# Storing the last tile of a per-sequence low-rank update in two transfers: 108 rows and 20 rows for 128

## The reference

```
B_sel = B[adapter_ids]
A_sel = A[adapter_ids]
Bx = jnp.einsum('bni,bri->bnr', x, B_sel)
out = jnp.einsum('bnr,bor->bno', Bx, A_sel)
return out * SCALING        # SCALING = 16.0 / 16
x = x + _L0_cond_ref(x, A, B, itok_B_3_7)
```

## Time and profile before

| | |
|---|---|
| median of three runs | 91.9 us (91.75 to 92.27) |
| the profiled execution, its own time | 92.17 us |
| its span, first to last instruction | 90.4 us |
| busy share of the span | TensorE 90%, GpSimd 70%, VectorE 66%, ACT 66% |
| DMA | 34.82 MB in 9297 packets, mean 385 GB/s |
| granted TensorE clock, mean | 0.973 |

### The profile page before, as it was taken

The page is one execution under the profiler, slowest core; times in us unless marked ns, Lnnn a source line. Parts: engine busy times, 40 slices in busy tenths (PEclk is TensorE's granted clock), DMA queues, the critical chain, the costliest instruction groups (busy, mean ns, idle before and its releaser), DMA issues.

```text
span 90.4 us, 3583 instructions
## 1 busy us (share of the span) xinstructions
PE 81.4 (90%) x1451; PEld 61.7 (68%) x1451; DVE 59.7 (66%) x111; ACT 59.5 (66%) x154; POOL 62.9 (70%) x141
## 2 busy tenths in 40 slices
PE   3998999989999999999999999999999999989200
PEld 3997778748786878787878787786868687443000
DVE  0309968276595868777686959595959595999000
ACT  1339869939696969696969695968687776542200
POOL 6103992999999998979696979797969792800000
PEclk9999999999999999999999999999999999999955
DMA  1999999999999999999999999999999999997980
GB/s 27 315 401 419 415 406 415 401 413 406 406 410 410 402 424 413 406 419 417 413 421 413 422 413 410 415 422 406 421 417 413 421 410 397 406 383 314 408 335 24
DMA packets 9297, 34.82 MB, mean 385 GB/s; under 512 B 450, under 2 KB 962, under 8 KB 9282
## 3 DMA queue, kind: packets, MB, share of 16 engines
q1 hardware_dynamic: 7552, 27.79, 76.8%
q10 hardware_dynamic: 1730, 6.82, 18.6%
HBM read 17.83 MB, written 16.78 MB: 383 GB/s over the span
## 4 chain that ended last, share of the span: by engine, by line
PE 82%; DMA 6%; ACT 4%; issue 1%
PE t_bank L255 35%; PE bx_bank L268 21%; PE y_banks L288 18%; DMA x_all<-in_A 6%; PE y_banks L315 2%; PE t_bank L319 2%; ACT x_all L365 1%; PE bx_bank L319 1%; ACT b_table L369 1%; PE y_banks L242 1%; PE bx_bank L315 1%; ACT x_all L424 1%; ACT x_t L377 1%; PE t_bank L315 1%; PE bx_bank L242 0%
## 5 line engine op out<-in xcount | busy, mean ns | idle before, releaser
L465 DVE TENSOR_TENSOR x_all<-y_banks,x_all 128x1024 f32<-128x1024 f32 x29 | 35.5, 1225 | 15.4 <-PE y_banks L288 15.0
L377 ACT COPY x_t<-t_bank 128x512 f32<-128x512 f32 x64 | 34.4, 591 | 13.6 <-PE t_bank L255 12.8
L198 POOL CAST a_duo<-a_table 128x512 fp32r x64 | 36.6, 613 | 3.5 <-PE y_banks L288 1.8
L255 PE MATMUL t_bank<-ident,x_all 128*128 128x128 f32 x256 | 35.0, 280 | 0.4 <-ACT x_t L377 0.4
L255 PEld LDWEIGHTS t_bank<-ident,x_all 128*128 128x128 f32 x256 | 27.4, 141 | 7.4 <-issue 5.2
L188 POOL COPY b_duo<-b_table 128x256 f32 x64 | 22.8, 399 | 6.0 <-PE bx_bank L268 6.0
L268 PE MATMUL bx_bank<-x_t,b_duo 128*32 128x64 f32 x1024 | 20.8, 222 | 0.0
L268 PEld LDWEIGHTS bx_bank<-x_t,b_duo 128*32 128x32 f32 x1024 | 15.8, 109 | 5.4 <-issue 5.4
L288 PE MATMUL y_banks<-a_duo,bx_parts 64*128 64x512 f32 x112 | 17.3, 420 | 0.3 <-issue 0.3
L456 DVE TENSOR_TENSOR bx_parts<-bx_bank,bx_parts 32x64 fp32r<-32x64 f32 x64 | 14.1, 220 | 1.4 <-ACT bx_parts L392 0.3
L392 ACT CAST bx_parts<-bx_bank 32x64 fp32r<-32x64 f32 x64 | 13.0, 204 | 1.9 <-PE bx_bank L268 1.3
(11 more groups left out here) (31 smaller groups left out, 22.2 us busy)
## 6 DMA issues: line engine op xcount, KB each, us to landing
x_all<-in_x SPq DMA_DIRECT2D x5, 2048.0 KB, 28.6
out_y<-x_all ACTq DMA_DIRECT2D x3, 2048.0 KB, 15.4
x_all<-in_x SPq DMA_DIRECT2D x4, 1024.0 KB, 14.0
out_y<-x_all SPq DMA_DIRECT2D x1, 3072.0 KB, 14.0
out_y<-x_all SPq DMA_DIRECT2D x6, 512.0 KB, 4.7
x_all<-in_x SPq DMA_DIRECT2D x4, 512.0 KB, 7.2
out_y<-x_all SPq DMA_DIRECT2D x1, 2048.0 KB, 9.7
out_y<-x_all SPq DMA_DIRECT2D x2, 1024.0 KB, 6.7
```

What stands on the lines that cost most here:

```text
L198: last = nc.gpsimd.tensor_copy(a_duo[duo % 2][:, k, :], a_table[:, bass.ds(adapters[k] * BANK, BANK)])
L255: last = nc.tensor.transpose(t_bank[unit % 2][:, c * P:(c + 1) * P], x_all[:, 2 * duo + tile, at:at + P], ident[:, :])
L377: nc.scalar.copy(x_t[duo % 2][:, half * HALF:(half + 1) * HALF, tile, :], t_bank[unit % 2][:, :].rearrange("p (c n) -> p c n", c=HALF)).th ...
L465: nc.vector.tensor_tensor(here, product, here, ALU.add).then_inc(y_drained, 1)
```

## The change

The store of tile 31 is issued as two transfers, rows 0 to 107 and rows 108 to 127, one right after the other on SP's queue; all other stores stay as they are. The last wait counts one transfer more.

```
--- before.py
+++ after.py
@@ -46,6 +46,7 @@
     LOADS += [(t, t + 4) for t in range(10, 30, 4)] + [(30, TILES)]
     STORES_BY_ACT = {4: (0, 4), 7: (4, 8), 10: (8, 12)}
     STORES = [(12, 18), (18, 22), (22, 24), (24, 26)] + [(t, t + 1) for t in range(26, TILES)]
+    LAST_STORE = [(0, 108), (108, P)]
     LOAD_OF = {tile: n for n, (first, end) in enumerate(LOADS) for tile in range(first, end)}
 
     ctx = ExitStack()
@@ -156,8 +157,10 @@
                     sp.wait_ge(y_drained, first)
                 if end == TILES:
                     sp.wait_ge(sum_copied, HALVES + 1)
-                sp.dma_start(out_rows[:, first:end, :], x_all[:, first:end, :]).then_inc(stored, 16)
-            sp.wait_ge(stored, 16 * (len(STORES) + len(STORES_BY_ACT)))
+                parts = [(0, P)] if end < TILES else LAST_STORE
+                for low, high in parts:
+                    sp.dma_start(out_rows[low:high, first:end, :], x_all[low:high, first:end, :]).then_inc(stored, 16)
+            sp.wait_ge(stored, 16 * (len(STORES) - 1 + len(LAST_STORE) + len(STORES_BY_ACT)))
 
         @block.gpsimd
         def _(pool):
```

## The result

The changed kernel is slower: 92.37 us in the median (92.25 to 92.69, 8 runs) against 91.89 us (91.61 to 92.27, 8 runs); ratio 1.0054, 95% interval 1.0039 to 1.0070, that is 0.50 us [0.36 to 0.64]. The forecast was 90.8 us; 92.37 is what the first rival gave (92.4).

What follows compares the result with a forecast made beforehand. TensorE and the DMA engines share the body; landing stores, with one late engine, bound the end. The wait ending at 88.76 instead of 90.0 gains 1.24 us on 92.17: 90.93, set at 90.8 us; 8-in-10 range 90.4 to 92.1.

Steps and rivals of the forecast that it cites:

- the first rival: Last store: the last engine is among the ten with 11 rows for 8, 0.47 us later, 92.4 us; chance 0.13.
- The dealing of the rows: Split last store: 108 rows go to 12 engines with 9 each, 20 rows to 10 with 2; four engines get none.
- The step that failed: Late engines at the kernel's end: taken as the four without rows, so the last drops 8 rows, 1.24 us.
- the good case: End of the stores: the four late engines get no rows, gain 1.24 us, 90.8 us; chance 0.66.
- the late engines are among those that get rows: Rival on the last store: the last engine takes 11 rows for 8, 0.47 us later, 92.4 us; chance 0.13.
- The second issue at 0: SP's queue at the end: one more store issue was taken to cost 0, with an upper bound of 0.43 us.
- Reads that hold each other up at 0: Two-row shares of the last store: mutual delay taken as 0, at most a doubling of those rows, 0.31 us.
- The cover named as thin: End of the stores: early engines land at 88.74, the late one at 88.76; over 0.05 us delay sets the end.
- the other limit: End of the stores: the late engine's limit, its wait ending at 88.76 instead of 90.0 once it drops 8 rows.

Runs made afterwards that it cites:

- 25 + 96 + 7: Last store split into three transfers of 25, 96 and 7 rows, against the kernel before the change: 92.55 us, ratio 1.0079.
- 17 + 96 + 15: Last store split into three transfers of 17, 96 and 15 rows, against the kernel before the change: 94.28 us, ratio 1.0256.
- 64 + 64: Last store split into two transfers of 64 rows each, against the kernel before the change: 91.98 us, ratio 1.0007.

## Why the prediction was wrong

- *The dealing of the rows*, 12 engines and then 10, was right: 456 small packets. The rule of the Trainium skill, page "DMA: Bandwidth & Descriptors", section "Why a DMA increments its semaphore by 16 and not by 1", agrees in the number; that narrow transfers always take the same, lowest-numbered engines fits the engines that got 9 + 2, 5 + 6 + 1 and 17 + 6 + 1 rows, while no run shows their numbers.
- *The step that failed* is "such a group is more likely to lie together at one end than to be scattered" and the leap behind it, that this end is the one left out. What the runs showed: the engine that ends last is one of the ten that both transfers use (11 rows, 1.71 us), and with 25 + 96 + 7 one of the first five. The forecast had said that no row numbers the engines and then gave the good case 0.66 because two groups were of the same size, four and four. That count was no evidence about where the group lies, and the group is not always of four: five engines were late in the changed kernel, two with 17 + 96 + 15, and there the first engine was neither of them. Whether it is always the same engines, and whether they lie together, stays open.
- *The rival* "the late engines are among those that get rows" was right in mechanism and price: 3 x 0.155 = 0.47, measured 0.50 [0.36 to 0.64]; equal shares give 0, four more rows (0.62) 0.66 to 0.75.
- *The second issue at 0* was right in its effect (64 + 64: 1.0007), though SP needed 1.08 us for both issues and not the some 0.7 us that the median of the earlier trace rows makes of two. That two transfers gain nothing, as the section "Rules for kernel authors" of the same page of the Trainium skill has it for halves, agrees with 64 + 64; at uneven shares the trace goes further, it loses.
- *Reads that hold each other up at 0* was too low. With twelve engines at work the rows moved at 262 GB/s (0.73 busy), 22 GB/s an engine for 26. The other nine of the ten closed between 88.78 and 89.21 us; the forecast had 88.27, or 88.68 in this execution, which is 0.41 us later. It cost nothing only because the last engine ends later still; that it would have eaten part of the gain, had the late ones been spared, is argued and not shown.
- *The cover named as thin* was never tested by the change, since the other limit did not move.

## What to carry to other kernels

Where the end is the landing of stores, count closings and busy engines in the last microseconds before cutting a transfer: one late engine can set the end while twelve stand idle. In this case the transfers that could not use all engines loaded some of the same engines each time, so an uneven split helps only if those are not the late ones. Read that from the closings and not from the time of a heavy load: 17 rows on one engine took 1.3 us more than 17 times 0.155, and the time looked like that of a late engine.

## What was not expected of the hardware

The issue of 108 + 20 rows kept SP for 1.08 us, against 0.33 to 0.43 us for one store of 128 rows; the two issues of 64 + 64 rows took 1.20 us, so the uneven counts are not the reason. Two transfers of 64 rows made all 16 engines slower than one of 128 (295 against 410 GB/s for a microsecond) without costing time. One engine with 24 rows took up to 0.59 us for one of them while it worked alone. And a wait that was already met cost TensorE 46 ns: 256 of them made 11.9 us, from 84.1 to 96.0 us.
